# The projection taken from the un-normalised sum with a centred W, and x added by TensorE or from 32x32 pieces

## The reference

```python
N, C = 4096, 128                                # x: [N, C], adj: [N, N]
def L0(x, evals, evecs, t):                     # evecs is adj
    x_spec = evecs.T @ x
    return evecs @ (exp(-evals * max(t[0], 1e-8))[:, None] * x_spec)
def L1(x1, adj, W, b):
    adj_hat = adj + eye(N)
    deg = adj_hat.sum(1, keepdims=True)
    return tanh((adj_hat / deg) @ (x1 @ W) + b)
x1  = layernorm(x + L0(x, evals, adj, t))       # no gain, no bias
out = layernorm(x1 + L1(x1, adj, W, b))
```

## Time and profile before

| | us |
|---|---|
| median of 3 runs (613.16 to 614.96) | 613.94 |
| the profiled execution | 615.71 |
| its span, first to last instruction | 613.9 |
| PE busy | 580.0 |
| DVE busy | 513.1 |
| ACT busy | 395.8 |
| POOL busy | 372.2 |
| mean granted TensorE clock | 0.986 of full |

### The profile page before, as it was taken

How to read it: one execution, slowest core, us unless ns; L and a number is a source line. 1 busy time by engine, 2 the same in 40 slices (tenths; PEclk the granted TensorE clock), 3 DMA queues, 4 the chain that set the end, 5 groups by cost and what they waited for, 6 DMA issues and landing times.

```text
span 613.9 us, 7978 instructions
## 1 busy us (share of the span) xinstructions
PE 580.0 (94%) x2454; PEld 445.5 (73%) x2454; DVE 513.1 (84%) x572; ACT 395.8 (64%) x854; POOL 372.2 (61%) x220
## 2 busy tenths in 40 slices
PE   5999999999998998899999999999999979999993
PEld 5888888888876565658888788887888855666562
DVE  4899999999899998798899798695776767999992
ACT  5999999999996656255655654555444523464653
POOL 0000000000157888589999999878887865787994
PEclk9999999999999999899999999999999989999997
DMA  8999999999999999689969999297994499999101
GB/s 307 410 409 407 409 408 409 408 409 409 408 315 335 327 331 343 176 235 301 264 179 264 254 296 282 64 256 190 258 258 138 130 345 346 347 343 309 30 18 52
DMA packets 125065, 174.67 MB, mean 285 GB/s; under 512 B 6884, under 2 KB 105700, under 8 KB 125032
## 3 DMA queue, kind: packets, MB, share of 16 engines
q1 hardware_dynamic: 72608, 121.68, 59.0%
q10 hardware_dynamic: 52424, 52.58, 30.5%
HBM read 172.13 MB, written 2.11 MB: 284 GB/s over the span
## 4 chain that ended last, share of the span: by engine, by line
PE 67%; POOL 13%; DVE 11%; issue 4%; ACT 3%; DMA 1%; ACTq 1%; DVEq 0%; POOLq 0%
PE ps L866 11%; PE ps L868 10%; POOL lo L488 10%; PE ps L867 10%; PE ps L838 9%; PE ps L839 9%; PE ps L840 9%; PE ps L862 6%; DVE vt L695 5%; DVE lo L676 1%; DVE lo L702 1%; ACT hi L543 1%; POOL rstd L467 1%; PE ps L823 1%; PE ps L928 1%
## 5 line engine op out<-in xcount | busy, mean ns | idle before, releaser
L488 POOL TENSOR_TENSOR lo<-vt,hi 128x1024 fp32r<-128x1024 f32 x123 | 309.5, 2541 | 45.9 <-ACT hi L543 45.4
L695 DVE STREAM_TRANSPOSE vt<-raw 128x1024 f32<-128x1024 f32 x184 | 222.1, 1226 | 63.9 <-PE ps L868 54.1
L543 ACT ACTIVATE hi<-vt 128x1024 fp32r<-128x1024 f32 x156 | 162.9, 1060 | 136.7 <-DVE vt L695 104.5
L676 DVE TENSOR_TENSOR lo<-raw,hi 128x1024 fp32r<-128x1024 f32 x124 | 158.0, 1279 | 15.9 <-ACT hi L529 7.9
L529 ACT ACTIVATE hi<-raw 128x512 fp32r<-128x512 f32 x256 | 158.8, 623 | 4.9 <-DMA raw<-in_adj_dram 1.8
L441 POOL TENSOR_TENSOR lo<-raw,hi 128x1024 fp32r<-128x1024 f32 x4 | 10.3, 2564 | 169.0 <-ACT hi L529 169.0
L866 PE MATMUL ps<-hi,s_hi 128*128 128x512 f32 x224 | 94.5, 422 | 8.8 <-POOL lo L488 5.9
L838 PE MATMUL ps<-hi,xg_hi 128*128 128x512 f32 x256 | 100.3, 392 | 1.4 <-DVE lo L676 1.4
L840 PE MATMUL ps<-hi,xg_lo 128*128 128x512 f32 x256 | 99.7, 389 | 0.0
L839 PE MATMUL ps<-lo,xg_hi 128*128 128x512 f32 x256 | 99.6, 389 | 0.0
L866 PE MATMUL ps<-hi,p_hi 128*128 128x512 f32 x200 | 88.1, 440 | 5.7 <-POOL lo L488 5.7
(11 more groups left out here) (69 smaller groups left out, 536.9 us busy)
## 6 DMA issues: line engine op xcount, KB each, us to landing
raw<-in_adj_dram SPq DMA_DIRECT2D x63, 1024.0 KB, 16.0
raw<-in_adj_dram SPq DMA_DIRECT2D x90, 512.0 KB, 9.8
raw<-in_adj_dram ACTq DMA_DIRECT2D x88, 512.0 KB, 11.9
late_raw<-in_adj_dram SPq DMA_DIRECT2D x8, 512.0 KB, 11.6
late_raw<-in_adj_dram ACTq DMA_DIRECT2D x8, 512.0 KB, 13.9
xn<-in_x_dram SPq DMA_DIRECT2D x8, 256.0 KB, 15.6
x_sb<-in_x_dram SPq DMA_DIRECT2D x8, 256.0 KB, 14.6
out_dram<-x_sb ACTq DMA_DIRECT2D x7, 256.0 KB, 3.1
```

The costliest lines, as they stand in the source:

```text
L488: nc.gpsimd.tensor_tensor(lo[:, slot(p), :], vt[:, slot(p), :], hi[:, slot(p), :].bitcast(f32), ALU.subtract).then_inc(pool_lo_ready, 1)
L543: nc.scalar.activation(hi[:, slot(s), :], vt[:, slot(s), :], ACT.Copy).then_inc(hi_ready, 1)
L676: nc.vector.tensor_tensor(lo[:, q % RING1, :], raw[:, k, 2 * h:2 * h + 2, :].rearrange("p r n -> p (r n)"), hi[:, q % RING1, :].bitcast(f3 ...
L695: nc.vector.transpose(vt[:, slot(s), :].rearrange("p (m a i) -> p m a i", m=2, a=RB), load_buffer(st.load).rearrange("p (a m e i) -> p e m ...
```

## The change

- W is centred once at the start: V = (I - 1/C) W. POOL makes `centre`, PE multiplies, DVE copies the result over `w_sb`. Of the 36 transposes of the identity 20 are left.
- Since a row's mean falls out with V, p = rstd * (h @ V), where h = x + L0. So PE multiplies h, not x1. ACT scales with rstd as it makes `p_hi` and `full`; `p_lo` is formed by four scalar_tensor_tensor. The transposes of x1 and the copies behind them (L922, L608) are gone.
- x is added before the transposes. For groups 0 and 1 PE adds it to the bank (four float32 matmuls with the identity, since -2). For the others DVE turns x in 32x32 pieces (since -3) and adds it as it copies the bank to `stage` (since 0). For groups 0 and 1 that copy is a plain one. It was ACT's before.
- ACT copies the transposed h to `x_sb` (since 2); the statistics are taken from there, all since 3. `p_hi` is made since 6 (before 11), `p_lo` since 7 (before 12), x1 and `full` since 8.
- The order of rows within a group changes: x comes in 4 DMAs per group (rows of 512 B for groups 0 and 1, pieces of 128 B, 2048 per group, for the others, where before 128 rows of 2 KB came in one). Each group is stored by 4 DMAs, SP and ACT two each. The degrees come back in 4 DMAs of 128 B rows (8 DMAs of 16 B pieces before), and DVE turns them once.

```diff
+    BY_PE = 2
+    PHI = 6
...
                 if n % NU == NU - 1 and g < NG:
-                    sp.dma_start(x_sb[:, g, :], x_v[g // 2, g % 2]).then_inc(x_in[g % 2], 16)
+                    for m in range(JB if g < BY_PE else 0):
+                        sp.dma_start(x_sb[:, g, m * C:(m + 1) * C], x_blocks[g // 2, g % 2, m]).then_inc(x_in[g % 2], 16)
+                    for b in range(QN if g >= BY_PE else 0):
+                        sp.dma_start(x_sb[b * QP:(b + 1) * QP, g, :].rearrange("i (a c) -> i a c", c=QP),
+                                     x_v[g // 2, g % 2, b]).then_inc(x_in[g % 2], 16)
...
+            nc.gpsimd.tensor_scalar_add(centre[:, :], ident[:, :], -1.0 / C).then_inc(centre_ready, 1)
...
@@ ending2 on ACT
-                if since == 1:
-                    act.wait_ge(mm_done, END2[g] + 1)
-                    nc.scalar.activation(stage[:, 0, :], acc2(g), ACT.Copy).then_inc(acc_out, 1)
-                if since == 7:
-                    normalise(acc2(g), g % 2, g, g, rs2, x1_ready)
-                if since == 9:
-                    act.wait_ge(x1T_done, g + 1)
...
-                if since == 11:
-                    act.wait_ge(xw_done, g + 1)
+                if since == 2:
+                    act.wait_ge(accT_done, g + 1)
+                    nc.scalar.activation(x_sb[:, g, :], acc2(g), ACT.Copy).then_inc(h_ready, 1)
+                if since == PHI:
+                    act.wait_ge(pw2, g + 1)
+                    act.wait_ge(hw_done, g + 1)
+                    for m in range(JB):
+                        last = nc.scalar.activation(p_hi[:, blocks(g, m)], acc2(g)[:, m * C:(m + 1) * C], ACT.Copy,
+                                                    scale=rstd[:, g % 2, m:m + 1])
+                    last.then_inc(phi_ready, 1)
+                if since == PHI + 2:
+                    normalise(x_sb[:, g, :], g % 2, g, g, rs2, x1_ready)
                     if g >= WHOLE_P:
+                        act.wait_ge(p_ready, g + 1)
+                        for m in (2, 3):
...
@@ ending2 on DVE
-                if since == 2:
-                    dve.wait_ge(accT_done, g + 1)
-                    dve.wait_ge(x_in[par], 16 * (g // 2 + 1))
-                    nc.vector.tensor_tensor(acc2(g), acc2(g), x_sb[:, g, :], ALU.add).then_inc(h_ready, 1)
+                if since == -3 and g >= BY_PE:
+                    dve.wait_ge(x_in[par], 16 * QN * (g // 2 + 1))
+                    nc.vector.transpose(stage[:, 1, :], x_sb[:, g, :]).then_inc(xT_ready, 1)
+                if since == 0:
+                    dve.wait_ge(mm_done, END2[g] + 1)
+                    if g:
+                        dve.wait_ge(hw_done, g)
+                if since == 0 and g < BY_PE:
+                    nc.vector.tensor_copy(from_blocks(stage[:, 0, :]), by_block(acc2(g))).then_inc(hT_ready, 1)
+                if since == 0 and g >= BY_PE:
+                    dve.wait_ge(xT_ready, g - BY_PE + 1)
+                    nc.vector.tensor_tensor(from_blocks(stage[:, 0, :]), by_block(acc2(g)), by_block(stage[:, 1, :]),
+                                            ALU.add).then_inc(hT_ready, 1)
                 if since == 3:
                     dve.wait_ge(h_ready, g + 1)
-                    row_stats(acc2(g), par, st2)
-                if since == 4:
+                    row_stats(x_sb[:, g, :], par, st2)
                     mean_and_var(par, g, st2, mv2)
-                if since == 12:
+                if since == PHI + 1:
                     dve.wait_ge(phi_ready, g + 1)
...
@@ PE
-            for _ in range(36):
+            pe.wait_ge(w_in, 16)
+            pe.wait_ge(centre_ready, 1)
+            nc.tensor.matmul(ps[:, NK - 2, :P], centre[:, :], w_sb[:, :], start=True, stop=True).then_inc(centred, 1)
+            for _ in range(20):
                 nc.tensor.transpose(ps[:, NK - 1, :P], ident[:, :], ident[:, :])
             pe.wait_ge(coef_ready, 1)
+            pe.wait_ge(wc_ready, 1)
...
             def ending2(g, since):
+                if since == -2 and g < BY_PE:
+                    pe.wait_ge(x_in[g % 2], 16 * QN * (g // 2 + 1))
+                    for m in range(JB):
+                        nc.tensor.matmul(by_block(acc2(g))[:, :, m], x_sb[:, g, blocks(0, m)], ident[:, :],
+                                         start=False, stop=False)
                 if since == 1:
-                    pe.wait_ge(acc_out, g + 1)
+                    pe.wait_ge(hT_ready, g + 1)
...
-                if since == 8:
-                    pe.wait_ge(x1_ready, g + 1)
-                    for r in range(R):
-                        last = nc.tensor.transpose(acc2(g)[:, r * P:(r + 1) * P], x_sb[:, g, r * C:(r + 1) * C],
-                                                   ident[:, :])
-                    last.then_inc(x1T_done, 1)
-                if since == 10:
-                    pe.wait_ge(x1T_ready, g + 1)
+                if since == 3:
+                    pe.wait_ge(h_ready, g + 1)
```

More of the change, by code:

```diff
@@ L308, in parts3, with blocks @@
             return [(range(R // 2), ps[:, bank, :], row + 1), (range(R // 2, R), ps[:, LATE3[0], :], row + 2)]
+        def blocks(g, m):
+            return slice((g * JB + m) * C, (g * JB + m + 1) * C)
         def columns(rows):
@@ L374, in load_quarters, with store @@
                               adj_q[ld.group // 2, ld.group % 2, ld.wide, q]).then_inc(block_in[ld.buf], 16)
+        def store(eng, row, count, odd):
+            g = ENDINGS[row]
+            for m in [ms for ms, _, n in parts3(row) if n == count][0][odd::2]:
+                eng.dma_start(out_v[g // 2, g % 2, m], x_sb[:, g, m * C:(m + 1) * C]).then_inc(stored, 16)
         blk = ctx.enter_context(nc.Block())
@@ L421, in _ @@
                     sp.wait_ge(deg_out, 16)
-                    for h in range(NG):
-                        sp.dma_start(rdeg[:, h, :], deg_by_group[h // 2, h % 2]).then_inc(deg_in, 16)
+                    for q in range(QN):
+                        sp.dma_start(rdeg_tile[q * QP:(q + 1) * QP].rearrange("p g r -> p (g r)"), deg_by_block[q])\
+                            .then_inc(deg_in, 16)
+            for row in range(NG):
+                for _, _, count in parts3(row):
+                    sp.wait_ge(out_ready, count)
+                    store(sp, row, count, 0)
         @blk.gpsimd
@@ L635, in ending3 @@
                         act.wait_ge(out_ready, count)
-                        act.dma_start(out_v[g // 2, g % 2][:, :, columns(rows_of)], x_sb[:, g, columns(rows_of)])\
-                            .then_inc(stored, 16)
+                        store(act, row, count, 1)
             for p in range(AHEAD, POSITIONS):
@@ L786, in ending3 @@
                                 out=bank[:, r * C:(r + 1) * C], in0=bank[:, r * C:(r + 1) * C],
[L787 removed]
+                                scalar=rdeg[:, g // 2, r, g % 2:g % 2 + 1], in1=b_bc[:, :], op0=ALU.mult, op1=ALU.add)
                         last.then_inc(pre3, 1)
@@ L883, in products @@
                     pe.wait_ge(p_ready, g - 1)
+                if first2 and g - 2 >= WHOLE_P:
+                    pe.wait_ge(full_ready, g - 1 - WHOLE_P)
                 if st.graph:
                     pe.wait_ge(p_ready, st.unit + 1)
+                    if whole(s):
+                        pe.wait_ge(full_ready, st.unit - WHOLE_P + 1)
                 if first3 and st.visit == NG and g in LATE3:
                     pe.wait_ge(p_ready, NG - 1 + LATE3[g])
+                    pe.wait_ge(full_ready, NG - 1 + LATE3[g] - WHOLE_P)
                 if carried:
@@ L937, in ending3 @@
                             pe.wait_ge(out_ready, ENDINGS.index(0) + 1)
-                        for r in rows_of:
-                            last = nc.tensor.transpose(bank[:, r * C:(r + 1) * C], spread(stage[:, row % 2, :], r),
+                        for m in rows_of:
+                            last = nc.tensor.transpose(bank[:, m * C:(m + 1) * C], stage[:, row % 2, m * P:(m + 1) * P],
                                                        ident[:, :])
                         last.then_inc(sumT_done, 1)
-            pe.wait_ge(w_in, 16)
             for p in range(AHEAD, POSITIONS):
```

71 lines of the change are left out of this document (42 added, 29 removed).

## The result

| | before | after |
|---|---|---|
| median of the runs | 614.45 | 643.76 (641.42 to 644.62) |
| ratio to before, 95% interval | | 1.0469, 1.0450 to 1.0488 |
| span of the profiled execution | 613.9 | 641.1 |
| mean granted TensorE clock | 0.986 | 0.974 |

29 us slower, where 4.6 us faster was forecast. They answer to the earlier trace rows.

What follows compares the result with a forecast made beforehand. PE was taken as the bound, busy 580 of 613.9 us. Group 0 +0.6, group 1 -0.1, wait for p -4.1, groups 4 to 7 -1.8, DVE +0.8: -4.6, so 609.3 us from 613.94, range 605.5 to 614.5.

Steps and rivals of the forecast that it cites:

- The DMAs: Loads of x for groups 2 to 7 in 128 B pieces: rate falls, but x is issued long ahead; taken as 0.
- The end: Last DMA is 64 KB in place of 128 KB, on two queues: 0, between -0.3 and +0.3 us.
- Rival 3: Small pieces hold up the load queues, up to 4 us per group, costing 8 in groups 2 and 3: 617.3 us; chance 0.12.
- wait for p: PE's 2.53 us wait for `p_lo` at 248.29 goes, and the half clock behind it: -4.1 us, between 0 and -4.1.
- x by PE, each: Groups 0 and 1: PE adds x by four float32 matmuls, +0.89 us each, possibly up to twice that.
- wait for the copy: PE's transposes at group ends wait for DVE's copy or add: group 0 +1.7, group 1 +0.9, group 5 +0.8 us.
- start: PE waits for W, then runs one matmul and 20 transposes: 0, between -0.5 and +0.6 us.
- rival 1: PE's clock falls at group 0's new wait for the copy: 611.8 us; chance 0.19.
- rival 2: Nothing is gained at 248 because something else holds that step, so the 4.1 us stay: 613.4 us; chance 0.10.
- waits of 1.57, 1.50 and 0.83: PE's waits for POOL's `lo` after groups 0, 1 and 5, used up by earlier statistics: -1.6, -1.5, -0.8 us.
- DVE's, sized +0.8: DVE's extra work, 7 us in all from `p_lo` pieces and turns of x: +0.8 us, between 0 and +4.

Runs made afterwards that it cites:

- experiment 7: Against the version with x and stores cut along q: PE adds x in all eight groups, not only groups 0 and 1; 615.02 us, ratio 1.0019.
- the last version: Version with x and stores cut along q, plus 28 start transposes before waiting for W, W copied after DVE's fourth `lo`, SP issuing all but last-row stores; 609.55 us.

## Why the prediction was wrong

**The step that failed is "The DMAs", which I took as 0.** It priced only the pieces of 128 B and passed over the other two edits: x of groups 0 and 1, which the change lists as rows of 512 B, and the stores, counted only for the last one's 64 KB in "The end". Size was the wrong question. The pieces of 128 B have an outermost step of 32. The rate does fall beside them, as at the row of the degrees. In the version with x and stores cut along q, x of group 2 is issued from 251.38 to 257.97 us, and over half of its 2048 pieces start in this stretch:

```profile
260.00:265.00 5.00, 5.00 (x24) 3.62 (x23) 4.48 (x12) 2.86 (x6) 4.84 (x6) 1.00 1.14 214
```

PE is busy for all of it. The next stretch stands at 201 GB/s, but there it is the degrees going out in 16 B pieces, and no piece of 128 B starts. Nobody waits for a load in either, so the 0 taken for the pieces held: the loads stand far enough ahead. It held for them alone. The eight DMAs of 512 B rows have an outermost step of 4 and cost 24.3 us, and the stores 6.8. Rival 3 had the mechanism by half (loads queued behind x on SP, a load landing later than its first turn, DVE waiting) but with the wrong DMAs, the wrong groups, a price of 8 and 0.12.

The shape stood in the diff. The source of x was written as `u e m q i c`, so with u, e and m fixed the first step left is q, with 4 places. I read from it the size of a row and not the outermost step. The lead was no cover either: x was issued early in both kernels, but what it delays is not itself. It delays the loads in flight beside and behind it, and before the change these run at 350 GB/s from 205 to 215 us, with the DMA share at 1.10. Slowed to 191 and 212, they landed up to 13.3 us after DVE was ready for them.

**The other steps**, read in the version with x and stores cut along q, where the DMAs don't hide them:

| step | forecast | measured |
|---|---|---|
| wait for p | -4.1 | gone; late p costs 4.6 to 6.2 |
| x by PE, each | +0.89 | 0.89 and 0.89 |
| wait for the copy, group 0 | +1.7 | 1.21 |
| group 1 | +0.9 | 0.41 |
| group 5 | +0.8 | 0.49 |
| start | 0 (-0.5 to +0.6) | +0.86 |
| the end | 0 (-0.3 to +0.3) | +0.35 |
| stage 3 | not in the sum | +1.5 |
| in all | -4.6 | -2.4 by medians, -3.4 by spans |

The time of x by PE is read from the chain; the run of experiment 7 was priced with 0.94, a little too much. By the interval of its ratio this version is 1.4 to 4.1 us faster than before: without the DMAs' cost the sum would still have been a little too good, by the start and by stage 3. The rows for the wait of group 0 and the start (the 20 transposes stand in two rows that overlap):

```profile
226.01 0.66 PE L997 MATMUL ps<-ident,stage 128*128 128x128 f32 x4 [1.21 <-DVE stage L820]
```
```profile
8.59 0.80 PE L888 MATMUL ps<-w_sb,centre 128*128 128x128 f32 x2 [1.40 <-DMA w_sb<-in_L_gnn_W_dram]
9.18 1.06 PE L891 MATMUL ps<-ident 128*128 128x128 f32 x4
9.60 4.00 PE L891 MATMUL ps<-ident 128*128 128x128 f32 x18
13.30 0.53 PE L907 MATMUL ps<-hi,xg_hi 128*128 128x512 f32 x1
```

So the mechanism of the waits was right, and the clock didn't fall behind the new wait, which was rival 1: it stands at 1.00 in every stretch of 5 us from 190 to 450. No wait for `p_lo` is left; rival 2 is out. The waits of 1.57, 1.50 and 0.83 that I took as used up are gone; two of 0.7 for POOL's `lo`, at 244.81 and 247.16, are new. By the transposes of group 7 this version is 5.3 us ahead of before (483.88 against 489.15), though it started 0.86 behind: up to there the computation gives about 6, more than the 4.6 forecast (one execution of each). Which part of the surplus is DVE's, sized +0.8, no run separates. It then loses 1.5 in stage 3, where ACT issues two stores for a part in place of one; the last version, with those stores on SP, gives that back. The start came out at or over its upper bound: W came as forecast, but the 20 transposes took 4.1, the upper end of what I allowed, and the product ahead of them 0.6. In this version the first product stands at 13.30, in the changed kernel as it was at 12.98, which is +0.5.

By the medians the stores cost 12.2 us in the changed kernel as it stands and 6.8 on the version with x cut along q. By the ratios it is 11.1 and 7.9, each known to 2 or 3 us. The old form that served for the first is also lighter on ACT, by some 3 us as the last version shows, so there may be nothing left between the two; no run settles it.

## What to carry to other kernels

Read the outermost step of every DMA that an edit rewrites (the runs here vary it on the side of HBM), before the size of its rows: a rearrangement that puts a dimension of 4 first changes nothing in bytes or in the packets of data, and cost 27 us here from 512 KB. A DMA's own lead doesn't protect the kernel; ask what is in flight beside it when the queues are at full rate. In a profile the sign is a DMA share at its top with the rate far down, and here issues of four small DMAs that take over ten us (with packets of 2 KB they took 4 to 5 us, and there was a cost all the same). Quicker to read is the count of packets under 512 B. Whether it costs time is told by the waits for loads, since much the same share and rate (1.14, 214 GB/s) cost nothing where the loads stood far ahead.

## What the runs showed that I had not expected

The outermost step and the size of the packets seem to work together. Four DMAs a group, by outermost step and packet size, in the kernel before:

| | outermost 16 | 8 | 4 |
|---|---|---|---|
| 2 KB packets, all groups | 614.18 | 615.49 | 625.33 |
| 512 B packets | 614.01 (all groups) | not run | 641.65 (groups 0 and 1 alone) |

On 16 the packet size makes no difference; on 4 the price goes from 11 us to 27, with a quarter of the DMAs. But the two runs on 4 differ in one thing more: each DMA of 2 KB packets writes 32 partitions, each of 512 B packets 128. That alone cost nothing on 16; on 4 no run takes the two apart, so that it is the packet size is not shown. The rule alone doesn't give the size of the cost. The rate of 348 GB/s is 21.8 per engine; four DMAs of 64 KB on 4 engines put 48 KB more on each than on 16, which is 2.3 us at that rate, and the measured price is some 13 us a group with 512 B packets. In the trace between 190 and 240 us a packet of 512 B takes 0.060 us on average in the changed kernel, against 0.036 in the kernel before with its x in 512 B packets on 16. On 4 engines a group's x is 128 packets each, so 7.7 us of their time; on 16 it is 32 packets and 1.2 us. This is an estimate from those numbers. It gives half of the 13 us. The rest is not settled: the DMA share stays at 1.15, so by this measure the other engines didn't stand idle while four worked, and the packets of the loads took longer too. Twice as wide (8) the cost is no longer measurable, so it isn't proportional.

The Trainium skill, "DMA: Bandwidth & Descriptors", section Specifications, gives 512 B as the size from which a transfer has full rate. The runs agree for 16 engines, where packets of 512 B cost no time (0.9994). On 4 the size doesn't tell the cost: 512 B and 2 KB are both within the limit, and both cost time, 27 us and 11.
